# Softmax denominators of a perceiver kernel: one reciprocal for four heads, through 32x32 block transposes

## What is computed

```python
def attention(x, kv_inp, g, wq, wkv, wo, out_g, null_kv, causal, attn_bias, freqs):
    xn = layernorm(x, g)
    kv = xn if kv_inp is None else kv_inp
    q = (xn @ wq) ...            # 16 heads of 64
    k, v = jnp.split(kv @ wkv, 2, axis=-1)   # one key and value head for all 16
    ...                          # rotary for self-attention; a null key and value ahead of the others
    q = l2norm(q) * math.sqrt(SCALE)
    k = l2norm(k) * math.sqrt(SCALE)
    sim = jnp.einsum('bhid,bjd->bhij', q, k) ...
    attn = jax.nn.softmax(sim)
    out = jnp.einsum('bhij,bjd->bhid', attn, v) ...
    return layernorm(out @ wo, out_g)

for l in range(L):
    x = attention(x, None, ...) + x        # self-attention, causal, with bias
    x = attention(x, context, ...) + x     # cross-attention over 2048 keys
    x = feedforward(x, ...) + x            # u * silu(gate) @ w2
```

## Time and profile before

| | |
|---|---|
| median of 3 runs | 3179.4 us (3177.19 to 3183.63) |
| the profiled execution | 3171.39 us |
| its span | 3169.6 us |
| TensorE matmuls busy | 2848.3 us (90%) |
| VectorE busy | 2734.6 us (86%) |
| ScalarE busy | 2159.3 us (68%) |
| GpSimd busy | 758.6 us (24%) |
| mean granted TensorE clock | 0.958 |

### The profile page before, as it was taken

The page is one execution under the profiler, slowest core; times in us unless marked ns, Lnnn a source line. Parts: engine busy times, 40 slices in busy tenths (PEclk is TensorE's granted clock), DMA queues, the critical chain, the costliest instruction groups (busy, mean ns, idle before and its releaser), DMA issues.

```text
span 3169.6 us, 49515 instructions
## 1 busy us (share of the span) xinstructions
PE 2848.3 (90%) x13204; PEld 1576.5 (50%) x13204; DVE 2734.6 (86%) x4914; ACT 2159.3 (68%) x3995; POOL 758.6 (24%) x488
## 2 busy tenths in 40 slices
PE   3699999999999999999999999999999999999856
PEld 1345545545545545545555555455455455455534
DVE  4599998999998998998998998998998998998665
ACT  2477777777777767767767777777777777777501
POOL 3312222223223223223123122132132122231000
PEclk7799999999999999999999999999999999999856
DMA  2000000000000000001001001001001001000000
GB/s 101 14 1 14 14 23 15 1 32 15 14 23 15 1 28 19 1 14 37 1 3 44 1 14 38 1 1 46 1 14 38 1 1 46 1 1 12 1 0 4
DMA packets 11333, 51.64 MB, mean 16 GB/s; under 512 B 1362, under 2 KB 6019, under 8 KB 6275
## 3 DMA queue, kind: packets, MB, share of 16 engines
q1 hardware_dynamic: 11012, 47.88, 4.3%
HBM read 47.58 MB, written 0.29 MB: 15 GB/s over the span
## 4 chain that ended last, share of the span: by engine, by line
DVE 36%; PE 27%; issue 22%; POOL 9%; ACT 5%; DVEq 1%; DMA 0%; ACTq 0%; SPq 0%; POOLq 0%
DVE PL L542 13%; PE psS L921 7%; DVE rden L527 6%; DVE rdens L527 5%; POOL rn L357 5%; PE psO L956 3%; PE psO L959 3%; PE psO L957 3%; PE psL L1002 2%; PE psL L1001 2%; DVE ss L486 2%; ACT PH L768 2%; ACT P L774 1%; POOL Psn L399 1%; DVE oTs L521 1%
## 5 line engine op out<-in xcount | busy, mean ns | idle before, releaser
L542 DVE TENSOR_TENSOR PL<-P,PH 128x512 fp32r<-128x512 f32 x1536 | 1160.5, 784 | 42.0 <-ACT P L774 31.7
L768 ACT ACTIVATE PH<-psS 128x512 fp32r<-128x512 f32 x1536 | 931.2, 606 | 313.5 <-PE psS L921 296.8
L774 ACT ACTIVATE P<-psS 128x512 f32<-128x512 f32 x1536 | 933.5, 608 | 183.7 <-DVE PL L542 181.0
L921 PE MATMUL psS<-QT,KT 128*128 128x512 f16 x3072 | 935.3, 387 | 28.3 <-issue 18.5
L956 PE MATMUL psO<-PH,V 128*128 128x512 f32 x1536 | 888.0, 578 | 0.8
L959 PE MATMUL psO<-PL,V 128*128 128x512 f32 x1536 | 610.3, 397 | 0.0
L957 PE MATMUL psO<-PH,VL 128*64 128x512 f32 x1536 | 606.8, 395 | 0.0
L921 PEld LDWEIGHTS psS<-QT,KT 128*128 128x128 f16 x3072 | 206.3, 98 | 422.2 <-issue 308.1
L956 PEld LDWEIGHTS psO<-PH,V 128*128 128x128 f32 x1536 | 294.0, 191 | 223.3 <-issue 52.8
L527 DVE RECIPROCAL rdens<-psL 64x128 f32<-64x128 f32 x384 | 357.7, 946 | 27.0 <-PE psL L1002 18.8
L527 DVE RECIPROCAL rden<-psO 64x128 f32<-64x128 f32 x384 | 364.6, 954 | 17.1 <-PE psO L953 6.6
(11 more groups left out here) (295 smaller groups left out, 3125.9 us busy)
## 6 DMA issues: line engine op xcount, KB each, us to landing
ctx_sb<-ctxT SPq DMA_DIRECT2D x24, 1024.0 KB, 4.8
W<-wpack SPq DMA_DIRECT2D x6, 1664.0 KB, 6.3
W<-wpack SPq DMA_DIRECT2D x6, 1280.0 KB, 5.6
ctx_sb<-biasM SPq DMA_DIRECT2D x1, 1024.0 KB
W<-tail_w SPq DMA_DIRECT2D x1, 832.0 KB
kraw<-biasW SPq DMA_DIRECT2D x1, 512.0 KB
ksq<-biasW SPq DMA_DIRECT2D x1, 512.0 KB
gsa<-gout SPq DMA_DIRECT2D x6, 64.0 KB, 6.4
```

The costliest lines, as they stand in the source:

```text
L542: nc_v.tensor_tensor(PL[:, here, :], P[:, slot(t, par, PSLOTS), :], PH[:, here, :], ALU.subtract).then_inc(sem("p_lo"), 1)
L768: nc_a.activation(PH[:, slot(s, par, HSLOTS), :], psS[:, s % SLOTS, :], ACT.Exp, scale=SIM_SCALE).then_inc(sem("p_hi"), 1)
L774: nc_a.activation(P[:, slot(s, par, PSLOTS), :], psS[:, s % SLOTS, :], ACT.Exp, scale=SIM_SCALE).then_inc(sem("ca_exp"), 1)
L921: ins = mm(bank[0:rows, :], keys[part], q, start=(part == 0), stop=(part == 1))
```

## The change

`evacuate` is replaced by `normalize`, and its 32 stages (one per head) by 32 others, four parts for each of the 8 groups: `spread` transposes the bank's denominators, 64 partitions x 512 columns, in blocks of 32x32 into `dens`, so that each column's denominator stands in a partition and the first column of each block has them all; `invert` takes the reciprocal of these 16 columns; `widen` transposes `rcol`, broadcast 32 times, back into the row `rrow`; `scale` makes two products of 64x256, even heads and odd heads. `dens` and `rrow` lie in partitions 64 to 127 of `rows_sb`. `ca_o` and `sa_o` now count 2 products a group. The table of VectorE is written anew for these stages, and `f_out` and `f_xnT_ca` are each one step later; the other tables are as before.

```diff
-        rows_sb = sb("rows_sb", [33, H * N])
+        rows_sb = sb("rows_sb", [128, H * N])
+        dens = rows_sb[64:128, 0:2 * QCOL].rearrange("p (k q) -> p k q", q=QCOL)
+        rrow = rows_sb[64:128, 2 * QCOL:4 * QCOL].rearrange("p (k q) -> p k q", q=QCOL)
-        rden = sb("rden", [64, 3, N])
+        rcol = sb("rcol", [128, 2, QCOL // 32])
-        rdens = sb("rdens", [64, 3, N])
...
-            25: ["b_silu", "f_sp1"], 27: ["f_se0", "f_se1", "e2"], 28: ["f_se2", "f_se3"], 29: ["b_act"],
-            32: ["f_se4", "f_se5"], 33: ["f_se6", "f_sp2"], 34: ["f_se7"], 36: ["e3", "f_se8"], 39: ["f_sp3"],
+            23: ["e_invert0"], 24: ["e_widen0", "f_sp0"], 25: ["b_silu", "f_sp1"], 27: ["e_scale0"],
+            29: ["b_act", "f_spread0"], 30: ["f_invert0"], 31: ["f_widen0"], 32: ["f_scale0"],
+            33: ["f_sp2", "f_spread1"], 34: ["f_invert1"], 35: ["f_widen1"], 36: ["f_scale1"],
...
-            def evacuate(tag, n, h, bank, rd, dst, pv_at):
+            def normalize(tag, at_, g, bank, dst, pv_at):
+
+
+                k = 0 if tag == "ca" else 1
+                cols, rc, rr = dens[:, k, :], rcol[64:128, k, :], rrow[:, k, :]
+
+                def spread(n, par):
+                    dve.wait_ge(sem(tag + "_pv"), pv_at(n))
+                    nc_v.transpose(cols, bank[64:128, :]).then_inc(sem(tag + "_den"), 1)
+
+                def invert(n, par):
+                    dve.wait_ge(sem(tag + "_den"), n * NG + g + 1)
+                    nc_v.reciprocal(rc, cols.rearrange("p (b c) -> p b c", c=32)[:, :, 0]).then_inc(sem(tag + "_inv"), 1)
+
+                def widen(n, par):
+                    dve.wait_ge(sem(tag + "_inv"), n * NG + g + 1)
+                    nc_v.transpose(rr, rc.unsqueeze(2).broadcast_to([64, QCOL // 32, 32])).then_inc(sem(tag + "_row"), 1)
+
+                def scale(n, par):
+                    dve.wait_ge(sem(tag + "_row"), n * NG + g + 1)
+                    for odd in range(2):
+                        nc_v.tensor_tensor(dst[64 * odd:64 * odd + 64, 2 * g:2 * g + 2, :],
+                                           bank[0:64, :].rearrange("p (c a n) -> p c a n", a=2, n=N)[:, :, odd, :],
+                                           rr.rearrange("p (c a n) -> p c a n", a=2, n=N)[:, :, odd, :],
+                                           ALU.mult).then_inc(sem(tag + "_o"), 1)
...
-                        pe.wait_ge(sem("sa_o"), n * H + GH * (g - 1))
+                        pe.wait_ge(sem("sa_o"), n * 2 * NG + 2 * (g - 1))
```

More of the change, by code:

```diff
@@ L251, in build @@
         PLAN_DVE = {
-            0: ["f_begin", "f_norm_sa"], 1: ["f_xnT_sa"], 3: ["b_e12", "b_e13"], 4: ["b_e14"], 6: ["f_V0", "f_V1"],
-            7: ["b_e15"], 8: ["f_ss_sa"], 11: ["f_V2"], 12: ["f_unit_sa"], 13: ["f_V3"], 15: ["b_out", "f_kss"],
-            17: ["b_xnT"], 18: ["f_null"], 19: ["f_kunit"], 22: ["f_KT_sa", "e0"], 23: ["e1"], 24: ["f_sp0"],
[5 rows of a table removed]
+            0: ["f_begin", "f_norm_sa"], 1: ["f_xnT_sa"], 3: ["b_spread3"], 4: ["b_invert3"], 5: ["b_widen3"],
+            6: ["f_V0", "f_V1"], 7: ["b_scale3"], 8: ["f_ss_sa"], 11: ["f_V2"], 12: ["f_unit_sa"], 13: ["f_V3"],
+            15: ["b_out", "f_kss"], 17: ["b_xnT"], 18: ["f_null"], 19: ["f_kunit"], 22: ["f_KT_sa", "e_spread0"],
[7 rows of a table added]
         }
@@ L513, in turned @@
                 return stage
-            def evacuate(tag, n, h, bank, rd, dst, pv_at):
[L518 to L531, removed]
+            def normalize(tag, at_, g, bank, dst, pv_at):
[17 more added lines that the diff above has]
+                                           ALU.mult).then_inc(sem(tag + "_o"), 1)
+                return {"spread": spread, "invert": invert, "widen": widen, "scale": scale}[at_]
             def core_step(s, core, back):
@@ L634, in _ @@
                 stages[f"f_KT{part}"] = f_KT(part)
[L635 to L639, removed]
+            for g in range(NG):
+                for part in ("spread", "invert", "widen", "scale"):
+                    stages[f"f_{part}{g}"] = normalize("sa", part, g, psL[:, g % 2, :], oTs, lambda n, g=g: n * NG + g + 1)
+                    stages[f"{'b' if g == NG - 1 else 'e'}_{part}{g}"] = normalize(
+                        "ca", part, g, psO[:, g % 2, :], oT, lambda n, g=g: (n * NG + g + 1) * CA_N)
             drive(dve, PLAN_DVE, stages, core_step)
@@ L949, in core_step @@
                 if j == 0 and (g >= 2 or not isinstance(n, int) or n > 0):
-                    pe.wait_ge(sem("ca_o"), n * H + GH * (g - 1))
+                    pe.wait_ge(sem("ca_o"), n * 2 * NG + 2 * (g - 1))
                 if is_null(t):
@@ L1009, in stage @@
                         pe.wait_ge(sem("w_back"), (n // B + 1) * 32)
-                    pe.wait_ge(sem(tag + "_o"), (n + 1) * H)
+                    pe.wait_ge(sem(tag + "_o"), (n + 1) * 2 * NG)
                     for c in range(H // 2):
```

## The result

The kernel became slower: 3232.1 us, median of four runs (3228.8 to 3234.8), against 3178.3 before (four runs, 3174.1 to 3183.6). The ratio is 1.0168, with a 95% interval of 1.0149 to 1.0186. The predicted 3170 and its range up to 3200 both missed. The profiled execution took 3231.5 us, its span is 3229.8 us, the mean granted clock 0.938 (before 0.958).

What follows compares the result with a forecast made beforehand. TensorE's work plus its waits was taken to bound the kernel. A window summed to -4.3 + 3.2 + 1.1 = 0.0 us, times 22, with 9 us gained outside: 3170 us predicted, range 3110 to 3200.

Steps and rivals of the forecast that it cites:

- the sum: Per window, -4.3 us gained, +3.2 new wait, +1.1 clock: 0.0, times 22; with 9 us outside, 3170 us.
- The clock: After the new wait at `f_sk2` TensorE very likely runs at the lower clock, costing 1.1 us a window (bounds 0 and 1.7).
- What bounds the kernel: In the loop, TensorE's work plus its waits make a window; only waits can be gained, not VectorE's busy share.
- The price of a group: On VectorE, a softmax group of four heads would cost 2.48 us in place of 4.95, each transpose 0.69.
- under 2300: Sign that the forecast is right: VectorE busy for under 2300 us.
- What is gained: TensorE's waits at the end of chains through VectorE, 4.45 us a window, would shrink by 4.3 us.
- The other four: TensorE's waits behind `KT`, `b_gate`, `f_wo` and `b_turn` would go like the largest one, as VectorE's backlog thins.
- What is added: TensorE's `f_sk2` would wait 3.2 us for group 0's products, now queued behind `b_act`, in 22 windows.
- some 7: Sign that the forecast is right: VectorE idle before `hu` for some 7 us, released by TensorE's `b_up`.
- The ends: Outside the 22 windows: 2.5 us gained at each of two output projections, some 4 in the second window, together 9.
- The new wait is not there: Rival: no wait at `f_sk2`, so 104 us less, 3075; chance 0.13.
- The fourth: Rival: the transpose costs 1.22 us, making the wait 4.3 and the time 3193, or a longer slow stretch; chance 0.20.

Runs made afterwards that it cites:

- a_ahead: The changed kernel with the four parts of the front's group 0 moved ahead of `b_act` in VectorE's table: 3099.4 us, ratio to before 0.9757.
- b_lowsmall: The kernel before, with GpSimd forming the low half of the cross-attention queries for one head of 16 only: 3147.4 us, ratio 0.9913.
- a_filled: The changed kernel with 13 useless matmuls on TensorE in front of its wait at `f_sk2`: 3159.8 us, ratio to before 0.9934.
- a_kt: The changed kernel with group 0's parts ahead of `b_act` and `f_KT1` moved to the front of step 60: 3093.7 us, ratio to before 0.9736.

## Why the prediction was wrong

By its own steps, a window came out at +2.88 us where the sum had 0.0. The waits that went are worth 1.80 us of idle time and not 4.3. The new wait is 3.04 and not 3.2. The clock costs 2.5 us more than before and not 1.1. And 0.9 us of busy time at full clock went, for which I had no term.

**What bounds the kernel: right.** The windows' time followed TensorE's busy time and waits, and VectorE's 313.5 us bought only what they took off these.

**The price of a group: right.** 2.52 us against 2.48; the transposes took 0.72 and 0.71 against 0.69. My reason for the 0.69, "every 4-byte operation here with an operand in PSUM runs at about one column per ns", was too wide: the reciprocal of 128 columns out of PSUM takes 0.95 us. VectorE's total fell by 380 us, not by the 470 that I gave, and "under 2300" of my last paragraph failed: 8 x 24 groups at 4.95 less 2.52 are 467, but the subtractions grew from 784 to 804 ns, 42 us in all. The other 45 us I did not trace.

**What is gained: wrong, the largest error.** I counted 4.3 us of 4.45. What the change gives with the order mended is 3.17 (before against `a_ahead`), and of this only 1.80 is idle time; the other 1.37 is busy time, of which I had not thought. Some 0.6 of it is clock: 37.5 us of the stretch were at the lower level before, 13.7 are now, mostly because slow stretches behind the waits at the loop's end are gone. The other 0.8 is busy time at full clock, spread over several rows (the transposes of line `L1054` took 49.4 us of the stretch before and 45.9 with the order mended); its cause is open. By the rows: `qs_all` gave 1.45 of its 1.69 (33.8 to 4.7 us over 20), near the 1.6 expected; `f_wo` all of its 0.57. `KT`, `b_gate` and `b_turn`, together 1.99 us of my sum, gave nothing: they stand at 22.5, 16.9 and 6.5 us, where 18.7, 15.2 and 5.9 were. The 0.2 us behind ScalarE's `P` stayed as well. The step that failed is the sentence "The other four are of the same kind: the copy `KT` stands behind a reciprocal and a product, `b_out` behind the backlog". It took what stands ahead in the queue for what is waited for. For `KT` the run `b_lowsmall` shows the real cause, GpSimd's operation of 2.15 us that the subtraction before the copy has to outlast. For `b_turn` and `b_gate` the held instructions are seen in two traces, and the run with `b_out` moved agrees, but no run took GpSimd's self-attention half away; so there it is read, not shown by itself.

The trace of before had it: its subtraction ahead of `KT` takes 1.70 us there too, where 0.69 is the rule, and ends 0.55 us after GpSimd's operation. I read the number 0.69 from one row and did not look for rows that differ.

```profile
1560.74 2.14 POOL L392 TENSOR_TENSOR qs_all<-qsq,qs_all 128x1024 f16<-128x1024 f32 x1 [2.65 <-ACT qs_all L781]
...
1561.73 1.70 DVE L542 TENSOR_TENSOR PL<-P,PH 128x512 fp32r<-128x512 f32 x1
```

The Trainium skill has it as well: the page "SBUF — State Buffer", section "SBUF: two separate sides", says that an operation of VectorE with two inputs in SBUF and one of GpSimd that reads SBUF exclude each other for the whole of an instruction, whichever started first. The trace agrees for the subtraction beside the low half, with 2.01 us. It does not agree beside GpSimd's power, which reads SBUF too: there the subtraction takes 0.68 us inside an operation of 3.56, so here the measurement decides, and the rule does not hold for every GpSimd operation. The page adds operations of VectorE in a 2-port mode; whether the TENSOR_SCALAR of 2.28 us ran in one, no row tells. With `KT`, `b_gate` and `b_turn` left in place, my gain would have been 2.3 us in place of 4.3, and the sum 3214 us (22 x 2.0 more than 3170).

**What is added: right.** 3.06 us, 20 times of 20, against 3.2, with the gaps of 0.03 us between the instructions. From `b_up`'s end to `f_sk2` were 5.62 us, against 5.65 predicted. VectorE's idle time ahead of `hu` was 5.04 us and not some 7, since it was not so far ahead at that point: the subtraction that starts at 1524.09, beside two operations of GpSimd, takes 3.25 us.

**The clock: wrong.** I took 1.1 us a window, with 1.7 as the upper bound; the slow stretches cost 2.8 us by `a_filled`, which fills the gap, and 3.0 by the busy time against `a_ahead`. Against the kernel before it is 2.5, since fewer of the waits at the loop's end are followed by a slow stretch (4 of 10 in place of 8). The bound came from one row, the stretch behind a wait of 2.56 us at the loop's end, 3.4 us at the lower level. Behind the wait at `f_sk2` it lasts 6.8 us in 14 of 20 windows, and nearly all of it lies on full work: the only idle time in the stretch shown above is the 0.69 us behind `Ps`. The argument that part of it would fall on waits holds for little: of the 153.6 us at the lower level TensorE is idle for 15.5. My statement that a wait of 1.7 us seldom brings the lower clock was right (2 of 20).

**The ends.** The span grew by 60.2 us, 57.7 of them in the 20 windows. With the two other windows of this kind at 2.88, 3.3 us were gained outside, where I had 9. The output projections' waits gave what I said, 5.11 and 5.2 fell to 2.7 and 2.8; the 4 us of the second window did not show.

**The rivals.** None had this cause, waits that are held by GpSimd and so stay. "The new wait is not there" put 3075 for a kernel without it; with the order mended it is 3099, for the missing gain. The fourth, which held "a longer slow stretch" beside the dear transpose, pointed the right way with 0.20, but its price, 3193, came from the transpose.

## What to carry to other kernels

A new wait of the bounding engine, the one whose work and waits make up the time, had to be paid nearly twice here: 3.06 us of idleness and 2.8 to 3.0 us of slower matmuls behind it. And a stage's place in a neighbour's queue (`f_spread0` behind `b_act`, which waits for TensorE itself) decided 133 us where the whole saving of VectorE's work is worth 75. So when an operation is split into parts or made cheaper, look first for what its parts stand behind, and move them ahead of any instruction that waits for the bounding engine. And before a wait is booked as gained because less work stands ahead of its end, compare the durations of the rows ahead of it with the same instruction elsewhere: one that takes 1.7 or 2.0 us where 0.69 is usual is held by another engine, and thinning the queue does nothing for it. A wait removed can come back as slow clock elsewhere (13.6 us of busy time in `a_kt`), so read TensorE's busy time beside its waits.

## What the runs showed of the hardware

*VectorE held by GpSimd.* A subtraction with both operands in SBUF that starts during GpSimd's subtraction of the low half ends after it: 2.01 us in place of 0.69 beside an operation of 2.15; 3.35 for two beside one of 2.75. A TENSOR_SCALAR with one operand in SBUF took 2.28 in place of 0.21. With GpSimd's operation at 0.31 us, the subtraction took 0.67. GpSimd's power, 2.90 or 3.56 us, lengthened none of the subtractions inside it; why it differs, no run here tells.

*How long the slow clock lasts.* Behind 3.06 us of idleness, with full work after it, the lower level stayed for 6.8 us in 14 cases and for 3.4 us in 6. Thirteen useless matmuls in the gap, at no other edit, took 72 us off the program.

*What stays open.* The waits at the loop's end (2.1 to 2.7 us) have nearly the same length in these kernels, but of those in the row "issue" slow matmuls follow in 7 of 8 cases before, in 4 of 10 in the changed kernel, and in 1 of 10 with the order mended; with `f_KT1` moved on top of that, they follow all 10. Why, no run here tells.

*The reciprocal's price goes by its columns.* 64x128 takes 0.95 us, 64x16 takes 0.245: 6.3 ns for each further column, against 1.0 ns of a product (0.284 us for 64x128, 0.418 for 64x256). This is why two transposes of 0.71 us and one short reciprocal pay for themselves in place of four reciprocals.
